# The first expert set's weights and the router's columns, loaded in the last slots of the first attention

## The chip, the cores and the metric

The kernel runs on one core of one Trainium2 chip. The metric is the device time of one execution in microseconds (us). The kernel before took 2045.58 us, the median of three runs (2042.79 to 2046.41). Times inside the kernel come from one profiled execution and are counted from the start of its span.

Five engines work beside each other, each with its own instruction stream: TensorE (PE; its weight loads are shown apart as PEld), VectorE (DVE), ScalarE (ACT), GpSimd (POOL) and SyncE (SP), which only issues transfers. A "q" behind a name (SPq, ACTq) marks the issuing of transfers and other work of that engine's sequencer. Engines wait for each other on semaphores.

## The reference, cut to what matters

Two layers run over x of 8 x 256 tokens x 512 features. Each layer is a gated cross attention and then a gated feed-forward part. The change lies between the first attention and the first feed-forward part:

```python
x = x + tanh(g_xattn[0]) * L0_xattn(layernorm(x), ctx, ...)   # 32 heads, rotary positions
x = x + tanh(g_ffn[0]) * L0_ffn(layernorm(x), ...)            # below
...                                                           # second attention, second routed part

def L0_ffn(x):                       # 2048 tokens, 16 experts, inner width 352
    probs = softmax(x @ w_gate.T)
    top_w, top_i = top_k(probs, 4)
    routed = sum over the 4 chosen experts e of  w_e * (silu(x @ wg[e]) * (x @ wu[e])) @ wd[e]
    shared = silu(x @ sg) * (x @ su) @ sd          # inner width 704
    return routed + shared
```

## The kernel before

**Two stages, one behind the other.** `rope_attention` computes the first attention and `expert_ffn` the first feed-forward part. Each is a block of five instruction streams, and between the blocks all engines meet at a barrier and the semaphores of the first are cleared. In the profile the last instruction of the first block ends shortly before 611 us and the first of the second starts at 612.5 us.

**The attention** runs through slots s = -21 to 132. Slots 0 to 127 each handle one pair of heads of one batch element (16 slots for each of 8 elements). Every engine's program is written out by hand as a loop over s, so the order of work on an engine is fixed by the code. In a slot, ACT copies a transposed tile out of PSUM (`turned_back`, L970), then computes the exponentials of the next pair (`exponentials`, L963), which wait for DVE's row maxima (`top`, L845). PE transposes exponentials (L1158) and computes scores (L1147). The last projection products of the last element (L1072) come in slots 120, 124, 128 and 131.

**Weight splitting inside the attention.** PE multiplies fp32 data as sums of fp32r parts, so every weight is split into a high and a low part. Eighteen sets (two halves of the shared expert, then 16 experts) are cut into 7 pieces each. SP loads a piece to `praw` (L551), POOL splits it (L671, L673) and SP writes both parts to the DRAM tensor `w_parts` (L559, L561). This goes on from slot 2 to the end of the attention. The pieces of set 0 are written first.

**The expert stage** works in units of 128 tokens: units 0 to 15 with set 0, 16 to 31 with set 1, and then 79 routed units. `wh` and `wl` hold high and low parts of three sets in SBUF. The streams at the start of this block are:

- SP: load the router's weights (`gw`, L1424); `weights(0)`: the gate columns of set 0, high and low (L1389), the rest of its rows (L1393) and the last 96 rows of the down weights (the tails, L1397); then zero rows, 17 clearing transfers for `slots`, and the copies of the normed tokens (L1439).
- ACT: issue a load of the routed map (L1715), wait for `gw` and write its high part beside the gate columns (L1742), then `tokens_high` (L1697) of units 0 and 1, then the logits' copy (L1708) and the silu (L1709) of unit 0.
- DVE: `normed(0)`, `normed(1)` (L1780), `dump_tokens` (L1973), `router_low` (L1787), `normed(2)`, `tokens_low(0)` (L1795), `normed(3)`, `tokens_low(1)`, some constants, and `acts(0)` (L1824).
- POOL: clear six tails of `wh` and `wl` (L1495), then `zero`, `empty` and `ent`, then an iota into `empty` (L1500), for which `dump_tokens` waits, and further constants.
- PE: `turn_tokens(0)`, `turn_tokens(1)` (L1575), `gate_products(0)` (L1605), `up_products(0)` (L1618), `turn_tokens(2)`, `gate_products(1)`, `turn_acts(0)` (L1627), `up_products(1)`, `down_products(0)` (L1638), and so on.

`gate_products(0)` waits for both gate transfers and for the router's parts; `up_products(0)` waits for the four transfers of rest and tails. `turn_tokens(1)` writes the PSUM tile that `tokens_low(0)` reads, and waits for it.

Of the kernel before, what the change touches and what calls it, by code (L numbers as in the profile page):

```python
# [15 lines left out]
P = 128  # L16
# [141 lines left out]
class Split:  # L158


    def __init__(self, nc, wg, wu, wd, sg, su, sd):
        self.wg, self.wu, self.wd, self.sg, self.su, self.sd = wg, wu, wd, sg, su, sd
        self.I = wg.shape[2]
        self.shared = sg.shape[1] // self.I
        self.sets = self.shared + wg.shape[0]
        self.rows = (self.I + P - 1) // P
        self.across, self.down = 2 * KD * self.I, self.rows * D
        self.each = KD + self.rows
        self.count = self.sets * self.each
        self.parts = nc.dram_tensor("w_parts", [self.sets, 2, P, self.across + self.down], F32, kind="Internal").ap()  # L170
        assert KD % 2 == 0 and 2 * self.I <= PIECE and D <= PIECE
# [134 lines left out]
def rope_attention(nc, core, x, ctx_d, pos, Wq, Wkv, Wout, bout, g_xattn, g_ffn, placing, table, split):  # L306
# [43 lines left out]
    SECOND_TOKENS = -1  # L350
    maps_W, atoms, eaw, importance, mask_idx = placing
# [45 lines left out]
    with ExitStack() as ctx:  # L397
# [3 lines left out]
        place_sums, place_rows = sb("place_sums", [P, C, E]), sb("place_rows", [P, C], U32)  # L401
# [3 lines left out]
        at_ = lies("atoms", [P, NS // 2], F32, nc.sbuf_base - 4 * KD * D)  # L405
        CS = sb("cs", [P, NT, 2, 2 * 8])
# [3 lines left out]
        xn = sb("xn", [P, BT, D])  # L410
        xT, cT = sb("xT", [P, KD, S]), sb("cT", [P, KC, S])
        rot, tmp = sb("rot", [P, 2, D]), sb("tmp", [P, 2, D])
        hlq, hlk = sb("hlq", [P, 2, H, 2, HD]), sb("hlk", [P, 2, H, 2, HD])
        qT, qS, kT = [sb(n, [P, QUADS, S], F32R) for n in ("qT", "qS", "kT")]
# [57 lines left out]
        phigh_done, plow_done = sem("phigh_done"), sem("plow_done")  # L472
        load_positions, angles, sines, tables = rope_tables(nc, ctx, pos, CS)
# [58 lines left out]
        kview = lambda a: a.rearrange("(k p) n -> p k n", p=P)  # L532

        @block.sync
        def _(eng):
# [184 lines left out]
        def _(eng):  # L720
# [235 lines left out]
        def _(eng):  # L956
# [59 lines left out]
            for s in range(FIRST, LAST):  # L1016
# [197 lines left out]
def expert_ffn(nc, core, w_gate, split, gate, Wq, Wk, Wv, Wkv_dca, Wo, table):  # L1214
# [3 lines left out]
    E, K, I = w_gate.shape[1], 4, split.I  # L1218
# [10 lines left out]
    GATE, UP, DOWN = KD * GE, KD * I, J * D  # L1229
    RAW = GATE + UP + DOWN  # L1230
    NW = 3
# [38 lines left out]
    with ExitStack() as ctx:  # L1270
# [11 lines left out]
        gw = sb("gw", [P, KD, E])  # L1282
# [39 lines left out]
        gw_in, gw_ready = sem("gw_in"), sem("gw_ready")  # L1322
# [20 lines left out]
        def columns(w, at, c, n):  # L1343

            if isinstance(at, int):
                return w[:, at, c:c + n]
# [11 lines left out]
        def loaded(eng, s):  # L1358

            eng.wait_ge(gate_in[s % NW], 32 * (s // NW + 1))  # L1360
            eng.wait_ge(rest_in[s % NW], 64 * (s // NW + 1))

# [14 lines left out]
        def _(eng):  # L1377
            def weights(s):
# [8 lines left out]
                for i, w in enumerate((wh, wl)):  # L1387
                    r, p_ = r32(w[:, s % NW, :]), split.parts[s, i]
                    eng.dma_start(r[:, 0:GATE].rearrange("p (k n) -> p k n", k=KD)[:, :, 0:I],  # L1389
                                  p_[:, 0:KD * I].rearrange("p (k n) -> p k n", k=KD)).then_inc(gate_in[s % NW], 16)  # L1390
                for i, w in enumerate((wh, wl)):
                    r, p_ = r32(w[:, s % NW, :]), split.parts[s, i]
                    eng.dma_start(r[:, GATE:GATE + UP + 2 * D],  # L1393
                                  p_[:, KD * I:2 * KD * I + 2 * D]).then_inc(rest_in[s % NW], 16)
# [29 lines left out]
            eng.dma_start(gw[:, :, :], w_gate.rearrange("(k p) e -> p k e", p=P)).then_inc(gw_in, 16)  # L1424
# [140 lines left out]
        def _(eng):  # L1565
# [116 lines left out]
        def _(eng):  # L1682
# [89 lines left out]
        def _(eng):  # L1772
# [9 lines left out]

            def router_low():

                eng.wait_ge(gw_ready, 1)
                pads = lambda w: w[:, 0, 0:GATE].rearrange("p (k n) -> p k n", k=KD)[:, :, I:GE]
                eng.tensor_tensor(pads(wl), gw[:, :, :], r32(pads(wh)),  # L1787
                                  ALU.subtract).then_inc(gw_ready, 1)
# [189 lines left out]
            router_low()  # L1978
# [1278 lines left out]
def program(nc, x, ctx_1024, fside_BxSx2_0, g_xattn, g_ffn, *args):  # L3257
# [6 lines left out]
    with ExitStack() as ctx:  # L3264
# [8 lines left out]
                       (W, atoms, atom_weights, importance, mask_idx), table, split)  # L3273
        Wq, bq, Wk, bk, Wv, bv, Wkv_dca, bkv_dca, *norms, Wo, bo = attn1
        expert_ffn(nc, core, ffn0[0], split, core.gates[:, 2:3], Wq, Wk, Wv, Wkv_dca, Wo, table)
# [35 lines left out]
```

## Time and profile before

| | us |
|---|---|
| median of three runs | 2045.58 |
| the profiled execution | 2045.0 |
| its span | 2043.3 |
| PE busy | 1836.0 (90%) |
| DVE busy | 1181.0 (58%) |
| POOL busy | 961.7 (47%) |
| ACT busy | 925.6 (45%) |
| mean granted clock of PE, as a share of full speed | 0.947 |

The span is the time from the first to the last instruction in the profile; the execution's own time is 1.7 us longer. Busy time is an average over stages with different limits. PE is the busiest engine, but a busy engine may run at the lower of its two clock levels (1.2 instead of 2.4 GHz), which the profile's PEclk shows as 0.50.

### The profile page before, as it was taken

What the parts mean: (1) busy time and instruction counts of PE and PEld (TensorE: products, weight loads), DVE (VectorE), ACT (ScalarE), POOL (GpSimd) and SP (SyncE); (2) the same over time, 40 slices, a digit from 0 to 9 for tenths busy, and PEclk for the clock granted to TensorE, in tenths of its full rate; (3) what the DMA queues carried; (4) which work ended last, traced back from release to release, by engine and by line L of the source; (5) the groups of instructions that cost most, each with busy time, mean ns of one, the idle gap of its engine ahead of it and who ended that gap; (6) DMA issues with size and microseconds to landing.
All of it is one profiled execution on the core that took longest, in us unless ns stands there. A gap on an engine that the chain in (4) does not pass through costs nothing. (4 is left out here: it accounts for less than half of the span.)

```text
span 2043.3 us, 38716 instructions
## 1 busy us (share of the span) xinstructions
PE 1836.0 (90%) x11488; PEld 1411.4 (69%) x11488; DVE 1181.0 (58%) x2665; ACT 925.6 (45%) x2631; POOL 961.7 (47%) x1018
## 2 busy tenths in 40 slices
PE   5889999999978999999999999994789999886992
PEld 3555666566547999999999999982455566555881
DVE  6866777677654875333333353325777778764445
ACT  5466767676642332233333333321466666640110
POOL 2557877788641364043333443322455555212660
PEclk9789999999998999999999999997899999996996
DMA  9677787778757246589999986533444545539657
GB/s 301 236 230 231 243 279 239 220 240 282 236 170 279 80 132 212 161 233 273 324 328 268 275 261 192 119 59 107 92 109 104 118 100 119 127 104 365 235 163 277
DMA packets 234941, 414.82 MB, mean 203 GB/s; under 512 B 44361, under 2 KB 121457, under 8 KB 228986
## 3 DMA queue, kind: packets, MB, share of 16 engines
q1 hardware_dynamic: 168250, 323.86, 49.7%
q0 software_dynamic: 30592, 62.54, 13.2%
q10 hardware_dynamic: 35904, 25.96, 4.2%
q8 instruction: 106, 1.74, 0.3%
q14 instruction: 89, 0.73, 0.1%
HBM read 211.97 MB, written 157.82 MB: 181 GB/s over the span
## 5 line engine op out<-in xcount | busy, mean ns | idle before, releaser
L963 ACT ACTIVATE a_P<-a_SC,a_nm 128x256 f32<-128x256 f32 x512 | 235.9, 473 | 151.5 <-DVE a_nm L845 150.9
L1543 POOL DMA_INDIRECT b_y_rows<-b_ysb,b_entry x79 | 125.0, 1582 | 334.8 <-ACT b_ysb L1691 185.0
L845 DVE TENSOR_REDUCE a_nm<-a_SC 128x2 f32<-128x512 f32 x256 | 164.7, 685 | 127.8 <-PE a_SC L1147 127.7
L673 POOL TENSOR_TENSOR a_praw<-a_praw,a_phigh 128x704 f32<-128x704 f32 (+2 forms) x126 | 193.8, 1538 | 10.3
L1795 DVE TENSOR_TENSOR b_xl<-b_XT,b_xh 128x512 fp32r<-128x512 f32 x97 | 67.0, 691 | 216.1 <-ACT b_xh L1697 215.7
L1158 PEld LDWEIGHTS a_T<-ident,a_P 128*128 128x128 f32 x1024 | 121.4, 146 | 86.5 <-issue 46.4
L1158 PE MATMUL a_T<-ident,a_P 128*128 128x128 f32 x1024 | 149.5, 285 | 26.8 <-DVE a_PT L857 24.1
L671 POOL CAST a_phigh<-a_praw 128x704 fp32r<-128x704 f32 (+2 forms) x126 | 106.5, 845 | 107.1 <-DMA a_praw<-in_L_ffn_wd 33.4
L1801 DVE TENSOR_TENSOR b_al<-b_AT,b_ah 128x384 fp32r<-128x384 f32 x111 | 61.8, 557 | 152.6 <-ACT b_ah L1702 152.6
L2529 ACT ACTIVATE c_P<-c_SC,c_nm 128x240 f32<-128x240 f32 x256 | 115.7, 457 | 75.6 <-DVE c_P L2400 75.6
L1691 ACT ACTIVATE b_ysb<-b_Y 128x512 f32<-128x512 f32 x79 | 47.3, 599 | 223.1 <-PE b_Y L1638 211.6
L1702 ACT ACTIVATE b_ah<-b_AT 128x384 fp32r<-128x384 f32 x111 | 54.6, 492 | 199.4 <-PE b_AT L1627 199.4
L1522 POOL DMA_INDIRECT b_slots<-b_ysb,b_at_u x64 | 65.5, 1023 | 105.3 <-DVEq L1888 87.0
L963 ACT ACTIVATION_READ_ACCUMULATOR a_P<-a_SC,a_nm 128x1 f32 x512 | 103.9, 203 | 0.0
L1530 POOL DMA_INDIRECT b_xg<-b_xn_rows,b_entry x79 | 78.3, 991 | 53.2 <-issue 22.5
L2394 DVE TENSOR_REDUCE c_nm<-c_SC 128x2 f32<-128x480 f32 x128 | 81.9, 640 | 36.7 <-PE c_SC L2704 36.2
L1638 PE MATMUL b_Y<-b_wh,b_ah 128*128 (+1 forms) x333 | 95.8, 396 | 0.9 <-ACT b_ah L1702 0.9
L1638 PE MATMUL b_Y<-b_wh,b_al 128*128 (+1 forms) x333 | 94.6, 392 | 0.0
L1638 PE MATMUL b_Y<-b_wl,b_ah 128*128 (+1 forms) x333 | 94.3, 391 | 0.0
L2714 PE MATMUL c_T<-ident,c_P 128*128 128x128 f32 x512 | 71.5, 281 | 24.5 <-POOL c_P L2321 15.5
L2714 PEld LDWEIGHTS c_T<-ident,c_P 128*128 128x128 f32 x512 | 57.4, 143 | 51.8 <-POOL c_P L2321 24.4
L1147 PE MATMUL a_SC<-a_kT,a_qT 32*128 32x256 f32 x512 | 82.5, 336 | 11.3 <-DMA a_qS<-a_qT 3.4
(496 smaller groups left out, 4916.4 us busy)
## 6 DMA issues: line engine op xcount, KB each, us to landing
w_parts<-a_phigh SPq DMA_DIRECT2D x72, 352.0 KB, 3.6
w_parts<-a_praw SPq DMA_DIRECT2D x72, 352.0 KB, 4.1
b_wh<-w_parts SPq DMA_DIRECT2D x18, 1216.0 KB, 10.9
b_wl<-w_parts SPq DMA_DIRECT2D x18, 1216.0 KB, 14.4
c_q<-c_qT SPq DMA_DIRECT2D x64, 256.0 KB
c_k<-c_kT SPq DMA_DIRECT2D x124, 128.0 KB
b_wh<-w_parts SPq DMA_DIRECT2D x18, 704.0 KB, 5.2
b_wl<-w_parts SPq DMA_DIRECT2D x18, 704.0 KB, 7.8
```

Source lines behind the costliest of these rows:

```text
L671: eng.tensor_copy(high[:, 0:k * m], raw[:, 0:k * m]).then_inc(phigh_done, 1)
L673: eng.tensor_tensor(raw[:, 0:k * m], raw[:, 0:k * m], r32(high[:, 0:k * m]), ALU.subtract).then_inc(plow_done, 1)
L845: eng.tensor_reduce(nm[:, g % 4, j, :], SC[j][:, :].rearrange("p (t k) -> p t k", t=BT), AX.X, ALU.max, negate=True).then_inc(topped, 1)
L963: e = eng.activation(Pr[:, i, t, :], SC[j][:, t * S:(t + 1) * S], ACT.Exp, bias=nm[:, g % 4, j, t:t + 1], accum_out=den[:, h, t:t + 1])
L1147: m = eng.matmul(SC[j][:, t * S:(t + 1) * S], q[r:r + R, p // 2, t * P:(t + 1) * P], kT[r:r + R, p // 2, :], start=(half == 0), stop=(half ...
L1158: m = eng.transpose(T_[j][:, k * S + t * P:k * S + (t + 1) * P], Pr[:, (2 * g + j) % NP_, t, k * P:(k + 1) * P], core.ident[:, :])
L1530: eng.indirect_dma_start(out=xg[:, row(v), :], out_offset=None, in_=xn_rows, in_offset=bass.IndirectOffsetOnAxis(ap=entry[:, r, 1:2].bitca ...
L1543: eng.indirect_dma_start(out=y_rows, out_offset=bass.IndirectOffsetOnAxis(ap=entry[:, r, 1:2].bitcast(U32), axis=0), in_=ysb[:, v % RING, ...
L1638: m = eng.matmul(Y[v % 2][:, :], a_[:, v % 2, j * P:(j + 1) * P], down_rows(w_, at_unit[v], j), start=(i == 0), stop=(i == 3 * J - 1))
L2394: eng.tensor_reduce(nm[:, g % 4, j, :, 0], v[:, :, 0:MAIN], AX.X, ALU.max, negate=True)
L2529: e = eng.activation(Pr[:, i, t, 0:MAIN], SC[j][:, t * S:t * S + MAIN], ACT.Exp, bias=nm[:, g % 4, j, t, 0:1], accum_out=den[:, h, t, 0:1])
L2714: m = eng.transpose(T[j][:, k * S + t * P:k * S + (t + 1) * P], Pr[:, (2 * g + j) % NP_, t, k * P:(k + 1) * P], core.ident[:, :])
```

## The change

The gate columns of set 0 and the rest of its rows without the tails (2 x 704 KB and 2 x 1216 KB) are no longer loaded at the start of the expert stage, but by ACT in slots 120 to 123 of the attention, one transfer in each. They go to the same SBUF addresses at which `wh` and `wl` of set 0 lie in the next block; in the attention these bytes hold projection weights, token tiles and other tensors that nothing reads any more by then. Tiles in the attention are laid out in another order for this. In slot 120 ACT also waits until the pieces of set 0 are written (semaphores that were reached long before) and issues the load of `gw`. In slot 124 ACT writes the router's high part, and in slot 125 DVE writes its low part. SP waits for the four transfers at the end of the attention. In the expert stage SP's load of `gw`, its four large transfers of set 0, ACT's wait and copy and DVE's `router_low` are gone, and PE's unit 0 waits only for the two tails. `dump_tokens` and POOL's clears stay as they are.

```diff
+                if s == FIRST_SET_AT:                       # ScalarE's stream in the attention; PAIRS * (B - 1) + 8 = 120
+                    is_freed(eng, (B - 1, "k1b"))
+                    n = split.each
+                    for i in range(NRAW):
+                        eng.wait_ge(plow_out[i], 16 * ((n - 1 - i) // NRAW + 1))
+                    for i in range(NHIGH):
+                        eng.wait_ge(phigh_out[i], 16 * ((n - 1 - i) // NHIGH + 1))
+                    eng.dma_start(gw[:, :, :], w_router.rearrange("(k p) e -> p k e", p=P)).then_inc(gw_in, 16)
+                if FIRST_SET_AT <= s < FIRST_SET_AT + 4:
+                    i, rest_ = (s - FIRST_SET_AT) % 2, s >= FIRST_SET_AT + 2
+                    if rest_:
+                        dst = r32(first_set[i][:, split.gate:split.raw - D])
+                        src_ = split.parts[0, i, :, split.up:2 * split.up + 2 * D]
+                    else:
+                        dst = r32(first_set[i][:, 0:split.gate]).rearrange("p (k n) -> p k n", k=KD)[:, :, 0:split.I]
+                        src_ = split.parts[0, i, :, 0:split.up].rearrange("p (k n) -> p k n", k=KD)
+                    eng.dma_start(dst, src_).then_inc(first_in, 16)
+                if s == ROUTER_AT:                          # FIRST_SET_AT + 4
+                    eng.wait_ge(gw_in, 16)
+                    eng.activation(router_columns(0), gw[:, :, :], ACT.Copy).then_inc(gw_high, 1)
...
+                if s == ROUTER_AT + 1:                      # VectorE's stream in the attention
+                    eng.wait_ge(gw_high, 1)
+                    eng.tensor_tensor(router_columns(1), gw[:, :, :], r32(router_columns(0)), ALU.subtract)
...
+            eng.wait_ge(first_in, 16 * 4)                   # SyncE, end of the attention
...
                 for i, w in enumerate((wh, wl)):            # SyncE in the expert stage, weights(s)
+                    if s == 0:
+                        break
...
+                    if s:
+                        eng.dma_start(r[:, GATE:GATE + UP + 2 * D],
+                                      p_[:, KD * I:2 * KD * I + 2 * D]).then_inc(rest_in[s % NW], 16)
...
-            eng.dma_start(gw[:, :, :], w_gate.rearrange("(k p) e -> p k e", p=P)).then_inc(gw_in, 16)
...
-                    eng.wait_ge(gate_in[v // NT], 32)       # TensorE, weights_at
+                    if v >= NT:
+                        eng.wait_ge(gate_in[v // NT], 32)
...
-                if v == 0:
-                    eng.wait_ge(gw_ready, 2)
...
-                    eng.wait_ge(rest_in[v // NT], 64)       # TensorE, up_products
+                    eng.wait_ge(rest_in[v // NT], 64 if v >= NT else 32)
...
-            eng.wait_ge(gw_in, 16)                          # ScalarE, before unit 0
-            eng.activation(wh[:, 0, 0:GATE].rearrange("p (k n) -> p k n", k=KD)[:, :, I:GE], gw[:, :, :],
-                           ACT.Copy).then_inc(gw_ready, 1)
...
             dump_tokens()                                   # VectorE, before unit 0
-            router_low()
```

## Rows read from the trace of the kernel before

**Rows 1.** Waits, all engines, 590 to 660 us: who waited for whom, total, times, longest.

```profile
PE b_XT L1575 <- DVE b_wl L1795: 4.9, 1, 4.9
ACT b_wh L1742 <- DMA b_gw<-in_L_ffn_w_gate: 12.0, 1, 12.0
PE b_U L1618 <- DMA b_wl<-w_parts: 3.9, 1, 3.9
```

**Rows 2.** Timeline of PE, 590 to 650 us: start, duration, instruction, idle before.

```profile
613.38 1.12 PE L1575 MATMUL b_XT<-ident,b_xg 128*128 128x128 f32 x4 [4.54 <-DVE b_xg L1780]
619.43 1.09 PE L1575 MATMUL b_XT<-ident,b_xg 128*128 128x128 f32 x4 [4.94 <-DVE b_wl L1795]
621.27 1.59 PE L1605 MATMUL b_G<-b_wh 128*128 128x368 f32 x4 [0.76 <-DMA b_wl<-w_parts]
...
629.09 1.54 PE L1618 MATMUL b_U<-b_wh 128*128 128x352 f32 x4 [3.92 <-DMA b_wl<-w_parts]
...
632.77 1.06 PE L1575 MATMUL b_XT<-ident,b_xg 128*128 128x128 f32 x4
633.49 1.58 PE L1605 MATMUL b_G<-b_wh 128*128 128x368 f32 x4
...
636.34 0.49 PE L1627 MATMUL b_AT<-ident,b_act 128*128 128x128 f32 x3
636.58 0.89 PE L1618 MATMUL b_U<-b_wh 128*128 128x352 f32 x4
...
638.60 0.85 PE L1638 MATMUL b_Y<-b_wh,b_ah 128*128 128x512 f32 x3
...
641.01 0.91 PE L1605 MATMUL b_G<-b_wh 128*128 128x368 f32 x4
...
643.11 0.49 PE L1627 MATMUL b_AT<-ident,b_act 128*128 128x128 f32 x3
```

**Rows 3.** Windows of 1 us: busy of PE, PEld, DVE, ACT, POOL; PEclk, DMA share, GB/s.

```profile
624.00:625.00 1.00, 1.00 (x5) 0.84 (x3) 0.00 (x0) 0.00 (x0) 0.00 (x0) 0.57 1.13 290
...
628.00:629.00 1.00, 0.00 (x0) 0.00 (x0) 0.00 (x0) 0.00 (x0) 0.00 (x0) 0.64 1.02 346
...
635.00:636.00 1.00, 1.00 (x8) 1.00 (x7) 0.19 (x1) 0.00 (x0) 0.00 (x0) 0.95 1.08 408
```

**Rows 4.** Timelines of POOL, DVE and ACT, 590 to 650 us.

```profile
617.62 0.21 POOL L1500 IOTA b_empty<- 128x16 int32 x1
...
617.86 0.26 DVE L1973 TENSOR_SCALAR b_empty<-b_empty 128x16 int32<-128x16 int32 x1 [3.80 <-POOL b_empty L1500]
...
618.61 0.67 DVE L1795 TENSOR_TENSOR b_wl<-b_XT,b_wh 128x512 fp32r<-128x512 f32 x1
...
617.30 0.26 ACT L1742 ACTIVATE b_wh<-b_gw 128x64 fp32r<-128x64 f32 x1 [12.00 <-DMA b_gw<-in_L_ffn_w_gate]
...
626.69 0.46 ACT L1709 ACTIVATE b_silu<-b_G 128x352 f32<-128x352 f32 x1
```

**Rows 5.** Waits of PE alone, 636 to 1100 us (the whole answer).

```profile
PE b_G L1605 <- issue: 0.6, 1, 0.6
```

**Rows 6.** Issues on SP's queue, 607 to 665 us.

```profile
612.51 0.41 SPq L1424 DMA_DIRECT2D b_gw<-in_L_ffn_w_gate  x1
...
613.52 1.27 SPq L1389 DMA_DIRECT2D b_wl<-w_parts  x1
```

**Rows 7.** Timeline of ACT, 566 to 593 us (slot 120 to 121).

```profile
574.25 0.61 ACT L970 ACTIVATE a_PT<-a_T 128x512 f32<-128x512 f32 x1
575.98 0.48 ACT L963 ACTIVATE a_P<-a_SC,a_nm 128x256 f32<-128x256 f32 x1 [1.12 <-DVE a_nm L845]
```

**Rows 8.** The longest issue on ACT's queue, from its timeline, 1250 to 1298 us.

```profile
1250.08 6.24 ACTq L1715 DMA_DIRECT2D b_mraw<-table  x1
```

**Rows 9.** PE and POOL, 566 to 613 us, and one window of 2 us.

```profile
581.24 0.63 PE L1158 MATMUL a_T<-ident,a_P 128*128 128x128 f32 x4 [1.48 <-DVE a_PT L857]
...
600.42 0.40 POOL L659 COPY a_recw<-a_rec 128x256 f32<-128x256 f32 x1 [3.50 <-DVE a_rec L852]
...
580.00:582.00 2.00, 0.63 (x4) 0.44 (x5) 1.18 (x3) 2.00 (x9) 1.57 (x1) 1.00 1.03 385
```

More of the change, by code:

```diff
@@ L169, in __init__ @@
         self.count = self.sets * self.each
+        self.gate_wide = self.I + wg.shape[0]
+        self.gate, self.up = KD * self.gate_wide, KD * self.I
+        self.raw, self.buffers = self.gate + self.up + self.rows * D, 3
         self.parts = nc.dram_tensor("w_parts", [self.sets, 2, P, self.across + self.down], F32, kind="Internal").ap()
@@ L303, in rope_tables, with rope_attention @@
     return load, angles, sines, tables
-def rope_attention(nc, core, x, ctx_d, pos, Wq, Wkv, Wout, bout, g_xattn, g_ffn, placing, table, split):
+def rope_attention(nc, core, x, ctx_d, pos, Wq, Wkv, Wout, bout, g_xattn, g_ffn, placing, table, split, w_router):
     H, HD = 32, 16
@@ L350, in rope_attention @@
     SECOND_TOKENS = -1
+    FIRST_SET_AT = PAIRS * (B - 1) + 8
+    ROUTER_AT = FIRST_SET_AT + 4
     maps_W, atoms, eaw, importance, mask_idx = placing
@@ L400, in rope_attention @@
         lies = lambda name, shape, dt, at: nc.alloc_sbuf_tensor_at("st_" + name, shape, dt, offset=at)
-        place_sums, place_rows = sb("place_sums", [P, C, E]), sb("place_rows", [P, C], U32)
+        first_set = [nc.alloc_sbuf_tensor_at(f"a_first_set{i}", [P, split.raw], F32R,
+                                             offset=nc.sbuf_base + 4 * i * split.buffers * split.raw) for i in range(2)]
+        core.first_set = first_set
+        first_main = 4 * (split.raw - D)
+        first_at = nc.sbuf_base
         wq, wkv, wo = sb("wq", [P, KD, D]), sb("wkv", [P, KC, 2 * D]), sb("wo", [P, KD, D])
@@ L405, in rope_attention @@
         at_ = lies("atoms", [P, NS // 2], F32, nc.sbuf_base - 4 * KD * D)
+        assert first_at + first_main <= wo_at
+        place_sums, place_rows = sb("place_sums", [P, C, E]), sb("place_rows", [P, C], U32)
         CS = sb("cs", [P, NT, 2, 2 * 8])
@@ L410, in rope_attention @@
         xn = sb("xn", [P, BT, D])
+        gw = lies("gw", [P, KD, w_router.shape[1]], F32, nc.sbuf_base - 4 * BT * D)
         xT, cT = sb("xT", [P, KD, S]), sb("cT", [P, KC, S])
         rot, tmp = sb("rot", [P, 2, D]), sb("tmp", [P, 2, D])
+        assert first_at + 4 * split.buffers * split.raw >= nc.sbuf_base - 4 * 2 * D
         hlq, hlk = sb("hlq", [P, 2, H, 2, HD]), sb("hlk", [P, 2, H, 2, HD])
+        assert first_at + 4 * split.buffers * split.raw + first_main <= nc.sbuf_base
         qT, qS, kT = [sb(n, [P, QUADS, S], F32R) for n in ("qT", "qS", "kT")]
@@ L472, in rope_attention @@
         phigh_done, plow_done = sem("phigh_done"), sem("plow_done")
+        first_in, gw_in, gw_high = sem("first_in"), sem("gw_in"), sem("gw_high")
         load_positions, angles, sines, tables = rope_tables(nc, ctx, pos, CS)
@@ L532, in rope_attention, with router_columns @@
         kview = lambda a: a.rearrange("(k p) n -> p k n", p=P)
+        def router_columns(i):
+            return first_set[i][:, 0:split.gate].rearrange("p (k n) -> p k n", k=KD)[:, :, split.I:]
         @block.sync
@@ L1211, in chosen_part, with expert_ffn @@
     eng.tensor_tensor(gt, a, b, ALU.is_gt).then_inc(sem, c.inc())
-def expert_ffn(nc, core, w_gate, split, gate, Wq, Wk, Wv, Wkv_dca, Wo, table):
-    E, K, I = w_gate.shape[1], 4, split.I
+def expert_ffn(nc, core, split, gate, Wq, Wk, Wv, Wkv_dca, Wo, table):
+    E, K, I = split.sets - split.shared, 4, split.I
     J = 3
@@ L1228, in expert_ffn @@
     GE = I + E
-    GATE, UP, DOWN = KD * GE, KD * I, J * D
-    RAW = GATE + UP + DOWN
-    NW = 3
+    GATE, UP, RAW, NW = split.gate, split.up, split.raw, split.buffers
+    assert GE == split.gate_wide and J == split.rows
     GT = 4
@@ L1281, in expert_ffn @@
         lnsc, lw = core.lnsc, sb("lw", [P, 5, NT])
-        gw = sb("gw", [P, KD, E])
         empty = sb("empty", [P, CLEAR, SLOT])
@@ L1321, in expert_ffn @@
         gate_in, rest_in, routed_in = sems("gate_in", NW), sems("rest_in", NW), sem("routed_in")
-        gw_in, gw_ready = sem("gw_in"), sem("gw_ready")
         mraw_in, high_out, low_out = sem("mraw_in"), sem("high_out"), sem("low_out")
@@ L1343, in columns @@
         def columns(w, at, c, n):
+            if isinstance(at, int) and at == 0 and c < GATE + UP + 2 * D:
+                return core.first_set[0 if w is wh else 1][:, c:c + n]
             if isinstance(at, int):
@@ L1358, in loaded @@
         def loaded(eng, s):
-            eng.wait_ge(gate_in[s % NW], 32 * (s // NW + 1))
-            eng.wait_ge(rest_in[s % NW], 64 * (s // NW + 1))
+            eng.wait_ge(gate_in[s % NW], 32 * (s // NW + (s % NW > 0)))
+            eng.wait_ge(rest_in[s % NW], 64 * (s // NW) + (64 if s % NW else 32))
         def token_parts(v):
@@ L1392, in weights @@
                     r, p_ = r32(w[:, s % NW, :]), split.parts[s, i]
-                    eng.dma_start(r[:, GATE:GATE + UP + 2 * D],
-                                  p_[:, KD * I:2 * KD * I + 2 * D]).then_inc(rest_in[s % NW], 16)
+                    if s:
+                        eng.dma_start(r[:, GATE:GATE + UP + 2 * D],
+                                      p_[:, KD * I:2 * KD * I + 2 * D]).then_inc(rest_in[s % NW], 16)
                     if s < 2:
@@ L1781, in normed @@
                                   ALU.mult, ALU.add).then_inc(xn_ready, 1)
[L1783 to L1788, printed above, removed]
             def tokens_low(v):
@@ L3272, in program @@
         rope_attention(nc, core, x, ctx_1024, fside_BxSx2_0, *attn0, g_xattn, g_ffn,
-                       (W, atoms, atom_weights, importance, mask_idx), table, split)
+                       (W, atoms, atom_weights, importance, mask_idx), table, split, ffn0[0])
         Wq, bq, Wk, bk, Wv, bv, Wkv_dca, bkv_dca, *norms, Wo, bo = attn1
-        expert_ffn(nc, core, ffn0[0], split, core.gates[:, 2:3], Wq, Wk, Wv, Wkv_dca, Wo, table)
+        expert_ffn(nc, core, split, core.gates[:, 2:3], Wq, Wk, Wv, Wkv_dca, Wo, table)
         core.Xa = ctx.enter_context(nc.sbuf_tensor("Xa", [P, NT, D], F32))
```

## The prediction

> **What bounds the kernel now.** I read the page first: PE is busy for 90% of the span, so time can be won only where PE stands still or runs slowly. The windows by stage put such a place at the start of the expert stage, and the waits there [rows 1] name three suspects: ACT's 12.0 us for the router's weights, PE's 4.9 us for DVE, and PE's 3.9 us for the weights of set 0. The 12.0 is a trap: it counts from ACT's last work in the attention, and since the transfer is issued only at 612.51 [rows 6] and ACT goes on at 617.30 [rows 4], no more than 4.8 us of it belongs to the load. What counts is PE's own timeline [rows 2]. After the barrier it transposes unit 0 at 613.38, stands until 619.43, transposes unit 1, starts the gate products at 621.27 when the low gate columns land, and after them stands 3.92 us until 629.09, when the low rest lands. Unit 0's up products then take until 632.77, and the first gate products of unit 1 until 636.34. From 636 to 1100 us PE waits for nothing but 0.6 us of issue [rows 5]. So what PE wins before 636 us should be kept through those units, since later loads hang on PE's own progress.
>
> The windows of 1 us [rows 3] add the clock. PE's granted clock is at half (1.2 GHz) when the gate products start, rises within 624 to 625 us (0.57 over that microsecond, so at about 624.9), while the gate products run, falls back in 628 to 629 us after the stall, and rises again at the very start of 635 us (0.95). The second stall therefore costs twice: the time itself, and half speed after it until 635.
>
> **Removed: the wait for gate columns and router.** PE may start the gate products of unit 0 when its tokens are split. That is where the first gain stops short. DVE writes the low tokens at 618.61, and before that in its program stands `dump_tokens`, which starts at 617.86 because POOL's iota starts only at 617.62 behind its clears [rows 4]. The change touches neither. The router's load ended at about the same moment by accident: ACT's wait and DVE's wait were late together, and with the first gone the second is there in full. All that goes from this chain is `router_low`, some 0.1 us. PE's transposes of unit 1 go from 619.43 to 619.3. At half clock the next products follow 0.72 us behind them (632.77 to 633.49 [rows 2]), so at 620.0 instead of 621.27. The gain so far is 1.25 us, not the 5 or so that the waits suggest.
>
> **Removed: the wait for the rest.** At half clock the up products take 629.09 to 632.77 = 3.68 us; the gate products with 368 columns for 352 take 3.68 x 368/352 = 3.85. They end at 620.0 + 3.85 = 623.9. The up products now wait for the two tails only (192 KB each). These wait for POOL's first two clears, over by 613.8, and have 10 us for what stood in one line with all of set 0 before. Cost nothing; if this cover is gone, each microsecond of lateness past 623.9 is lost.
>
> **The clock.** In the trace the rise at 624.9 came 5.5 us after PE's work began at 619.43, and the rise at 635.05 came 6.0 us after 629.09. PE now works without a pause from 619.3, with more work before 624.9 than it had, so I take the rise at the same 624.9. The up products do 1.0 of their 3.68 us at half clock, and the rest at full speed: 2.02 us for all (636.58 to 638.60), so 0.73 x 2.02 = 1.47. They end at 626.4 instead of 632.77. The transposes of unit 2 take half of 0.72, so unit 1's gate products start at 626.7, and at full speed take 2.10 us (641.01 to 643.11) for 2.85 (633.49 to 636.34 [rows 2]). They end at 628.8 instead of 636.34: **7.5 us** saved. Nothing else is late there: the silu of unit 0 ended 2.0 us after its gate products [rows 2, 4], so at 626.0, and DVE's 0.5 us behind the up products is done at 627.2, before PE wants it at 628.8. Had the clock stayed low until 635 as well, U and G of units 0 and 1 would end at 623.9 + 3.68 + 0.72 + 3.85 = 632.2, a gain of 4.1 us. Had it risen at 623, another 0.95 us would come.
>
> The Trainium skill (TensorE: Matmul & The Clock Gate, What's actually happening) says that the gate's moment of change depends on where the first matmul falls and varies from run to run. The rows agree in that the two rises come 5.5 and 6.0 us after work starts; by that rule the rise may come about half a microsecond to either side, which moves the sum by some 0.25 us, since half of each microsecond at half clock is lost.
>
> **Added in the attention.** Five issues, some ten waits that are long met, one ACT copy and one DVE subtraction. Slot 120's exponentials end just before 574.25, and the issues stand behind them and ahead of the copy L970 [rows 7]. What queues behind them on ACT is that copy and then the next exponentials, for which DVE and PE wait. But these exponentials start 1.12 us later than they could, waiting for DVE. So up to 1.1 us per slot is hidden. Slot 120 holds the router's issue (0.41) and one gate issue; large issues took 0.50 to 1.27 on SP [rows 6]. I take 0.41 + 0.50 + 0.4 for the waits = 1.3, so 0.2 shows, and 0.5 to 0.9 in slots 121 to 123, which is hidden. In those slots PE also has idle time of 1.48 us before its transposes, which end in a wait for DVE [rows 9]. ACT's copy (0.26) lies in an idle stretch. DVE's subtraction (0.22) is on the chain that PE waits for: 0.1 to 0.2. Together 0.5 us; bounds 0 and, if each issue holds as long as the worst in the trace (6.24 [rows 8]), 4 x (6.24 - 1.1) = 20.6 us. I take the low end, since SP issued these same transfers back to back, with 1.27 for the one shown [rows 6], and here they are 3.6 us apart. A gain below nothing is not excluded either: slots' ends shift against the clock's changes, some 1 us to either side.
>
> **The bytes.** 3840 KB, 3.9 MB, move into 574 to 590 us. At the 385 GB/s of a full window [rows 9] that is 10.2 us of transfer time. The pieces share the engines: their loads and stores get later, SP and POOL with them. POOL's last widened denominators had been free to start 3.50 us earlier [rows 9]; and the block ends only near 611. So a lag of 3.5 us is free for POOL. The four transfers start in four slots, 1.8 to 3.2 us of work each in 3.6, and the pieces' last loads come after 590, when these are done. Cost 0.
>
> The Trainium skill (DMA: Bandwidth & Descriptors, Issuing engines are not separate DMA queues) says that transfers from ScalarE run on the same 16 engines as SyncE's and interleave, so another issuer saves only issue time. It speaks against the change where the share is full, as in 580 to 582 us [rows 9]; by it all 10 us of them come on top of the pieces' traffic, and what does not fit in idle windows shows as POOL's lag.
>
> **The sum.** 7.5 - 0.5 = 7.0 us off the profiled execution's 2045.0, which gives 2038.0. It lies 0.6 under the median of 2045.58; on that median the forecast is 2038.6 us.
>
> **Rivals.** (a) Full gain: POOL's clears and `dump_tokens` don't hold DVE, and the token split follows the first transposes. These end at 614.5, and with ACT's and DVE's 1.3 us the second transposes start at 616, 3.3 us sooner; the gain is 11, the time 2034.8. For it: the 12.0 and 4.9 of [rows 1]. Against it: the program order and 617.86 [rows 4]. (b) Small gain: the clock rises later, or tails land after 623.9, with what remains of 7.5 near 4.1 to 5: 2041. For it: two periods of half clock in the trace; against it, that continuous work should not make the rise later. (c) Nothing: issue holds or a late POOL eat 4 to 10 us in the attention: 2042 to 2048. (d) Slower: ACT's issues in slots 121 to 123 hold as in [rows 8], because the pieces keep the DMA engines full (1.03 in 580 to 582). The price is 3 x (6.24 - 1.1) = 15.4 us less 7.5: 2053.5. It decides from a hold of 3.6 us in each slot on. Against it: the same transfer took 1.27 us to issue from SP [rows 6], a third of the hold that decides.
>
> **How the numbers follow.** My forecast, with 2036.5 to 2040.8 as its own range, gets 0.72; (a) 0.04; (b) 0.11; (c) 0.08; (d) 0.05. The range of 2035.0 to 2042.0 leaves out (d), most of (c) and part of (a). What a measurement of this kernel tells from no change is about 0.2%, 4.1 us, so a time under 2041.5 is faster: 0.72 + 0.04 + most of (b) and a little of (c) = 0.87. Within 0.2%: 0.08. Slower: 0.05.
>
> **What would show it.** In the changed kernel DVE's `dump_tokens` still starts 5.4 us after the block's start and `tokens_low(0)` right behind it; PE's gate products of unit 0 start 7.5 us after the block's start (8.8 before), the up products follow without a wait, and PEclk rises once within them and stays. Unit 0's L1627 comes 16.3 us after the block's start instead of 23.8. The attention's last instruction ends within 1 us of 610.8. A block that ends over 3 us later, or ACT issues above 1.3 us each, would prove (c) or (d); PE starting the second transposes before 617 would prove (a). A second fall of the clock before L1627 of unit 0 would prove (b).

## The result and the profile after

| | before | after |
|---|---|---|
| median of five runs | 2045.58 us | 2032.25 us (2031.29 to 2038.17) |
| ratio | | 0.9942, interval 0.9922 to 0.9962 |
| profiled execution, span | 2045.0, 2043.3 | 2031.29, 2029.6 |
| expert block's first instruction | 612.5 | 606.6 |
| from there to unit 0's L1627 (L1670 after) | 23.8 | 15.3 |

The kernel is 13.3 us faster by the medians, 8 to 16 by the interval; 7.0 were forecast, and the time lies below the forecast range. It is nearest to rival (a)'s 2034.8, but what rival (a) needed did not happen, as the lines below show. The last two rows of the table already say where to look: the start of the expert block gave 8.5 us, and 5.9 us were there before it began; behind both, 0.7 us were lost again.

PE after, timeline (start, duration, instruction, idle before). This answers to [rows 2]:

```profile
607.45 1.12 PE L1619 MATMUL b_XT<-ident,b_xg 128*128 128x128 f32 x4 [4.56 <-DVE b_xg L1820]
613.35 1.09 PE L1619 MATMUL b_XT<-ident,b_xg 128*128 128x128 f32 x4 [4.79 <-DVE b_wl L1828]
614.09 2.80 PE L1648 MATMUL b_G<-a_first_set,b_wh 128*128 128x368 f32 x8
...
617.46 1.45 PE L1661 MATMUL b_U<-a_first_set,b_wh 128*128 128x352 f32 x8
...
619.40 0.60 PE L1619 MATMUL b_XT<-ident,b_xg 128*128 128x128 f32 x4
619.76 1.59 PE L1648 MATMUL b_G<-a_first_set,b_wh 128*128 128x368 f32 x8
...
621.86 0.49 PE L1670 MATMUL b_AT<-ident,b_act 128*128 128x128 f32 x3
```

Both stalls for transfers are gone, and from 613.35 on PE does not stop. The wait that stays is the one for DVE, and behind it stands the order that the forecast named: POOL's iota, `dump_tokens`, the token split, as in [rows 4]. `dump_tokens` starts 5.3 us after the block's start (5.4 forecast).

```profile
611.68 0.21 POOL L1544 IOTA b_empty<- 128x16 int32 x1
...
611.92 0.26 DVE L2006 TENSOR_SCALAR b_empty<-b_empty 128x16 int32<-128x16 int32 x1 [3.79 <-POOL b_empty L1544]
...
612.53 0.67 DVE L1828 TENSOR_TENSOR b_wl<-b_XT,b_wh 128x512 fp32r<-128x512 f32 x1
```

The clock, in a window of 1 us (PEclk is the third number from the end), answers to [rows 3]. The value is 0.50 before this window, 0.54 in it and 1.00 after it, so the clock rises once, at about 616.9:

```profile
616.00:617.00 1.00, 1.00 (x5) 1.00 (x5) 0.08 (x2) 0.00 (x0) 0.00 (x0) 0.54 0.78 262
```

In the attention, ACT's issues and the exponentials of the slot after the first of them (compare [rows 7]):

```profile
565.96 0.43 ACTq L1071 DMA_DIRECT2D st_gw<-in_L_ffn_w_gate  x1
...
566.43 0.52 ACTq L1080 DMA_DIRECT2D a_first_set<-w_parts  x1
...
568.62 0.47 ACT L986 ACTIVATE a_P<-a_SC,a_nm 128x256 f32<-128x256 f32 x1 [0.97 <-DVE a_nm L865]
...
569.22 0.39 ACTq L1080 DMA_DIRECT2D a_first_set<-w_parts  x1
...
573.26 0.34 ACTq L1080 DMA_DIRECT2D a_first_set<-w_parts  x1
...
576.72 0.34 ACTq L1080 DMA_DIRECT2D a_first_set<-w_parts  x1
```

No issue took more than 0.52 us, and the issues lie beside the exponentials in the profile, not between them: ACT's sequencer ran ahead of its arithmetic. The exponentials still waited 0.97 us for DVE, against 1.12 before. From ACT's PSUM copy in slot 120 to the one in slot 128 it is 29.6 us, and it was 29.9. So no cost is seen there. The pieces did give way. POOL's last copy, which had waited 3.50 us for DVE [rows 9], now has no wait at all: POOL stood 4.23 us for the load of an earlier piece. The copy comes 1.7 us after ACT's last PSUM copy (592.87), where before it came 0.1 us ahead of it, so the free 3.5 us were used up and more. PE takes up the denominators at 596.64, without a wait:

```profile
587.91 0.61 POOL L691 CAST a_phigh<-a_praw 128x512 fp32r<-128x512 f32 x1 [4.23 <-DMA a_praw<-in_L_ffn_wd]
...
594.53 0.39 POOL L679 COPY a_recw<-a_rec 128x256 f32<-128x256 f32 x1
...
596.64 0.38 PE L1216 MATMUL a_O<-ident,a_recw 128*128 128x128 f32 x2
```

### The profile page after: what moved, and what is told of

Read it like the earlier page. It is cut to its first block and busy times, and to the rows that moved or that the text cites. A ratio compares the mean times of both kernels' runs of the same rounds, so it can differ in the third digit from the quotient of the medians.

```text
span 2029.6 us, 38719 instructions
## 1 busy us (share of the span) xinstructions
PE 1825.5 (90%) x11488; PEld 1403.7 (69%) x11488; DVE 1181.2 (58%) x2665; ACT 925.7 (46%) x2631; POOL 961.4 (47%) x1018
## 3 DMA queue, kind: packets, MB, share of 16 engines
q8 instruction: 106, 1.74, 0.3%
## 5 line engine op out<-in xcount | busy, mean ns | idle before, releaser
L693 POOL TENSOR_TENSOR a_praw<-a_praw,a_phigh 128x704 f32<-128x704 f32 (+2 forms) x126 | 193.4, 1535 | 10.3
L1681 PE MATMUL b_Y<-b_wh,b_ah 128*128 (+1 forms) x301 | 88.3, 396 | 0.9 <-ACT b_ah L1745 0.9
L877 DVE COPY a_PT<-a_T 128x512 f32<-128x512 f32 x128 | 87.0, 680 | 1.0 <-PE a_T L1201 1.0
L1681 PE MATMUL b_Y<-b_wh,b_al 128*128 (+1 forms) x301 | 87.4, 392 | 0.0
## 6 DMA issues: line engine op xcount, KB each, us to landing
b_wl<-w_parts SPq DMA_DIRECT2D x17, 1216.0 KB, 13.8
```

Of the source, the lines that this page charges most:

```text
L693: eng.tensor_tensor(raw[:, 0:k * m], raw[:, 0:k * m], r32(high[:, 0:k * m]), ALU.subtract).then_inc(plow_done, 1)
L877: eng.tensor_copy(PT[:, 2 * g % NPT, :, :].rearrange("p t s -> p (t s)"), T_[0][:, :]).then_inc(pt_done[0], 1)
L1681: m = eng.matmul(Y[v % 2][:, :], a_[:, v % 2, j * P:(j + 1) * P], down_rows(w_, at_unit[v], j), start=(i == 0), stop=(i == 3 * J - 1))
```

## The experiments

In what follows "the part" is the time from the expert block's start to unit 0's transposed activations: 23.8 us before, 15.3 with the change.

**The changed kernel again, twice** (no edit; the second time beside `dump_again` and `warm` below).

> The changed kernel once more, unchanged. In its first profile the expert block started 5.9 us earlier than before the change (606.6 for 612.5), and the gain was made before slot 120, where PE's clock was at half in four stretches (17 us in all between 115 and 552 us) before the change and in none after. Theory 1 (chance): these stretches come and go from run to run; this profile shows a block start anywhere from 606 to 613 us, times from 2031 to 2038 us, and the part from the block's start to unit 0's transposed activations stays at 15.3 us (14.5 to 16.5). Theory 2 (the new placing of tiles in the attention makes it quicker): the block starts at 606 to 607 again, and all times lie near 2032 us.

> The changed kernel, a third time, beside the two below on one chip. By the two profiles so far: 15.3 to 15.4 us from the expert block's start to unit 0's transposed activations and 1423 to 1424 us from there to the end of the span; the block's start anywhere from 606 to 613 us. Median 2035 to 2038 us.

The medians were 2037.83 (ratio 0.9954, 0.9937 to 0.9971) and 2035.26 us (0.9950, 0.9932 to 0.9968), beside 2046.27 and 2045.14 for the kernel before in the same rounds. The block started at 612.6 and at 611.8, not at 606.6, with the same program. The windows of 105 to 545 us, in which the change adds or removes no instruction, show the granted clock that goes with it: of before, of the first profile after, and of the two repeats, in this order.

```profile
105.00:545.00 440.00, 418.48 (x3167) 265.56 (x3168) 309.13 (x609) 304.88 (x1049) 328.30 (x299) 0.98 0.78 242
```

```profile
105.00:545.00 440.00, 416.34 (x3208) 265.05 (x3200) 312.65 (x616) 309.14 (x1066) 333.50 (x303) 1.00 0.79 245
```

```profile
105.00:545.00 440.00, 416.77 (x3181) 264.56 (x3175) 310.28 (x612) 305.35 (x1055) 328.56 (x300) 0.99 0.78 241
```

```profile
105.00:545.00 440.00, 417.64 (x3168) 264.43 (x3168) 309.06 (x611) 305.25 (x1053) 328.60 (x300) 0.98 0.78 241
```

In the same 440 us the first profile got through more instructions (3208 matmuls for 3167) at a clock of 1.00. The 41 matmuls more are 5.7 us at the rate of before (an estimate: 3167 in 440 us). So the 5.9 us are chance of that execution.

What one fall of the clock costs can be read where the program is the same. In the first repeat the clock is at half from about 599.3 to 602.7, in the second it is not, and PE's four projection products show it:

```profile
599.26 3.56 PE L1115 MATMUL a_W<-a_wo,a_aT 128*128 128x512 f32 x4
```

```profile
600.12 1.88 PE L1115 MATMUL a_W<-a_wo,a_aT 128*128 128x512 f32 x4
```

From slot 128's PSUM copy to the block it is then 13.7 us instead of 12.1. In the profile of before, the clock is at half for four such stretches between 106 and 506 us, 3 to 7 us each; in the first profile of the change there is none in 105 to 541 us.

The second repeat is also a close copy of the forecast, since here the clock rose late:

```profile
618.56 1.09 PE L1619 MATMUL b_XT<-ident,b_xg 128*128 128x128 f32 x4 [4.79 <-DVE b_wl L1828]
619.30 2.80 PE L1648 MATMUL b_G<-a_first_set,b_wh 128*128 128x368 f32 x8
...
628.10 0.49 PE L1670 MATMUL b_AT<-ident,b_act 128*128 128x128 f32 x3
...
624.00:625.00 1.00, 1.00 (x6) 1.00 (x6) 0.00 (x0) 0.99 (x2) 0.00 (x0) 0.80 0.70 239
```

The part is 628.1 - 611.8 = 16.3 us, which is the number forecast, with a rise at 624.4, 12.6 us after the start (12.4 assumed).

**Only the placing of tiles.** The kernel before, with the attention's tiles in the changed order:

```diff
+        first_set = [nc.alloc_sbuf_tensor_at(f"a_first_set{i}", [P, split.raw], F32R, offset=...) for i in range(2)]
-        place_sums, place_rows = sb("place_sums", ...), sb("place_rows", ...)   # ahead of wq, wkv, wo
+        place_sums, place_rows = sb("place_sums", ...), sb("place_rows", ...)   # behind them
```

> The kernel before with nothing but the tiles of the attention in the changed order; all loads stay where they were. Theory 1 (chance): the time is that of before, 2043 to 2047 us, the block's start varies with the half-clock stretches, and from there to unit 0's transposed activations it takes 23.8 us. Theory 2 (placing): the block starts near 606.6 us and the kernel takes 2039 to 2040 us.

Median 2047.74, ratio 1.0002 (0.9985 to 1.0018); the block starts at 614.1, and the part is 23.0 us. The placing gives nothing, and theory 2 is out. The part is 0.8 us shorter than in the profile of before with the same stage program: here the clock did not rise within the gate products but 4.1 us into the work behind the second stall (6.0 before). So the 23.8 itself varies by about that much.

**Only the gate columns and the router moved.** The two rests are loaded by SP in the expert block again.

```diff
-                if FIRST_SET_AT <= s < FIRST_SET_AT + 4:
+                if FIRST_SET_AT <= s < FIRST_SET_AT + 2:
...
-                    if s:
-                        eng.dma_start(r[:, GATE:GATE + UP + 2 * D], ...)
+                    dst = r[:, GATE:GATE + UP + 2 * D] if s else r32(core.first_set[i][:, GATE:GATE + UP + 2 * D])
+                    eng.dma_start(dst, ...)
```

> Of the changed kernel, only the two gate loads (704 KB each) and the router stay in the attention; the two transfers of the rest (1216 KB each) go back to SyncE in the expert block. If each wait is worth what the rows say: gate products start 7.5 us after the block's start, PE then waits 1 to 2 us for the low rest, which lands some 4 us sooner than before since 1.4 MB are gone from ahead of it (12.8 us after the start for 16.6), and unit 0's activations are transposed about 17 to 18 us after the start: 2 us slower than the whole change, 6 faster than before. Rival: the rest lands as late as before (16.6), because the bytes behind it take the freed time; then the clock falls again and the kernel is 6 to 7 us slower than the whole change.

Median 2039.51, ratio 0.9967 (0.9953 to 0.9982). The block starts at 612.4:

```profile
625.37 2.71 PE L1660 MATMUL b_U<-a_first_set,b_wh 128*128 128x352 f32 x8 [1.39 <-DMA b_wl<-w_parts]
...
631.15 0.49 PE L1669 MATMUL b_AT<-ident,b_act 128*128 128x128 f32 x3
```

The up products start at 12.9 us (12.8 expected), and the part is 18.7: 5.1 us less than before. That is a little later than expected, because the clock rose only after this short wait, at about 628.2, 15.8 us after the start. The part is 3.3 us longer than in the first two profiles of the whole change and 2.4 longer than in the third, for a wait of 1.39 us.

**Only the rests and the router moved.** The mirror image: SP loads the gate columns in the expert block.

```diff
-                if FIRST_SET_AT <= s < FIRST_SET_AT + 4:
+                if FIRST_SET_AT + 2 <= s < FIRST_SET_AT + 4:
...
-                    if s == 0:
-                        break
-                    r, p_ = r32(w[:, s % NW, :]), split.parts[s, i]
+                    r, p_ = r32(w[:, s % NW, :]) if s else r32(core.first_set[i][:, :]), split.parts[s, i]
```

> Of the changed kernel, the two rests (1216 KB each) and the router stay in the attention; the two gate loads (704 KB each) go back to SyncE at the start of the expert block. If unit 0's start is held by the token split behind GpSimd's clears, the gate columns, now first in an empty line, are there by 7.5 us after the block's start, and all is as in the whole change: gate products at 7.5, unit 0's activations transposed at 15.3 us, 8.5 less than before. Rival: the gate loads themselves take 8.8 us as before, the gate products start at 8.8 and unit 0's activations are transposed at 16 to 17.

The block starts at 608.65.

```profile
617.35 2.82 PE L1645 MATMUL b_G<-a_first_set,b_wh 128*128 128x368 f32 x8 [0.85 <-DMA a_first_set<-w_parts]
...
626.16 0.49 PE L1667 MATMUL b_AT<-ident,b_act 128*128 128x128 f32 x3
```

The rival was right: PE starts on the gate columns 8.7 us after the block's start, even though they are first in SyncE's line and the rests are gone, and the part is 17.5 (16 to 17 expected). The median was 2039.61, ratio 0.9987 (0.9968 to 1.0005), too wide to tell by itself. The halves of the change give 5.1 and 6.3 us of the part, both together 7.5 to 8.5. They overlap: either half alone leaves one clock rise where there were two, 15.8 and 13.8 us after the start (22.6 before), and both together bring it to 10.3 to 12.6.

**Only the order, no move.** The kernel before, with the first token split ahead of everything that waits for POOL or for the router's load.

```diff
                 normed(v)
-            dump_tokens()
-            router_low()
...
                     tokens_low(u + 2)
+                if u == -2:
+                    dump_tokens()
+                    router_low()
```

(and ScalarE's wait for `gw` with its copy behind its first `tokens_high`).

> The kernel before (all loads in the expert block), with VectorE's dump_tokens and router_low behind the first token split, and ScalarE's wait for the router behind its first tokens_high, so that neither GpSimd's clears nor the router's load holds the split of unit 0. If set 0's loads are by then the bound: second transposes at 3.5 us after the block's start, gate products at 8.8 still, unit 0's activations at 23 to 24, time as before. If the clears were all that held it: gate products near 4.2 and 3 us or more gained.

Median 2045.6, ratio 1.0000 (0.9980 to 1.0019). The block starts at 610.2:

```profile
613.66 1.09 PE L1575 MATMUL b_XT<-ident,b_xg 128*128 128x128 f32 x4 [1.50 <-DVE b_wl L1796]
619.16 1.60 PE L1605 MATMUL b_G<-b_wh 128*128 128x368 f32 x4 [4.41 <-DMA b_wl<-w_parts]
...
634.12 0.49 PE L1627 MATMUL b_AT<-ident,b_act 128*128 128x128 f32 x3
```

The second transposes come 3.5 us after the start instead of 6.9, and the time goes straight into the wait for the gate columns (9.0 us after the start; 8.8 before). The part is 23.9. Before the change there were two waits, one hidden behind the other.

**The order on top of the change**, run twice: `dump_tokens` moves behind the first token split, as above.

> The changed kernel with VectorE's dump_tokens moved from ahead of tokens_low(0) to right behind it, so that the first token split no longer stands behind GpSimd's clears. If that wait was what held the gate products: PE's second transposes start about 3.5 us and the gate products 4.2 us after the block's start instead of 7.5, and the kernel is 1.7 to 3.3 us quicker than the whole change, by how early the clock rises. If the first split was held by something else, the start stays at 7.5 and the time is that of the whole change.

> The kernel with dump_tokens behind the first token split, a second time: 11.9 us to unit 0's transposed activations, 1419 to 1420 us from the block's start to the end, and a median 2 to 4 us below the changed kernel's in the same rounds. If the 3 us between the first medians were chance, the part of the block is 11.9 again but the medians are equal.

Medians 2034.73 (ratio 0.9947, 0.9928 to 0.9966) and 2032.08 (0.9937, 0.9912 to 0.9962): 3.1 and 3.2 us below the changed kernel in the same rounds. The first profile, whose block starts at 611.1:

```profile
614.60 1.09 PE L1619 MATMUL b_XT<-ident,b_xg 128*128 128x128 f32 x4 [1.50 <-DVE b_wl L1828]
615.34 2.79 PE L1648 MATMUL b_G<-a_first_set,b_wh 128*128 128x368 f32 x8
...
623.05 0.49 PE L1670 MATMUL b_AT<-ident,b_act 128*128 128x128 f32 x3
```

Gate products at 4.2 us, part 11.9 us; in the second profile 4.2 and 12.9 (11.9 expected), with the clock rising 3.4 and 5.6 us after the second transposes began. What gave nothing alone gives 3.1 us once the loads are out of the way. It is the fastest of the versions in its own rounds. The intervals against the kernel before overlap with the changed kernel's; that it beats it rests on two pairs of medians and on the part.

**The loads twice.** In slots 124 to 127 ACT issues the four transfers again, to the same places.

```diff
+                if FIRST_SET_AT + 4 <= s < FIRST_SET_AT + 8:
+                    i, rest_ = (s - FIRST_SET_AT) % 2, s >= FIRST_SET_AT + 6
+                    if s == FIRST_SET_AT + 4:
+                        eng.wait_ge(first_in, 16 * 4)
...                                                  # dst and src_ as in the change
+                    eng.dma_start(dst, src_).then_inc(first_in, 16)
```

> The changed kernel with the four loads issued a second time by ScalarE, in slots 124 to 127, to the same places: 3.9 MB more through the last slots. From the PSUM copy of pair 119 to that of pair 127 the profiles show 29.9 us before, 29.6 and 29.9 with the change, and from there to the expert block 12.0 or 13.7. If issues and bytes are free there: 29.6 to 30.0 and 12.0 to 13.8 again. If the bytes cost by sharing the DMA engines with the weight pieces: the pieces' last loads, GpSimd's last copy and the block's start come 2 to 6 us later.

The block starts at 622.45. POOL's last piece and copy, then PE's products that need that copy:

```profile
605.64 0.61 POOL L691 CAST a_phigh<-a_praw 96x512 fp32r<-96x512 f32 x1 [5.03 <-DMA a_praw<-in_L_ffn_wd]
...
607.53 0.39 POOL L679 COPY a_recw<-a_rec 128x256 f32<-128x256 f32 x1
...
608.02 0.66 PE L1227 MATMUL a_O<-ident,a_recw 128*128 128x128 f32 x2 [3.45 <-issue]
608.61 3.64 PE L1234 MATMUL a_O<-a_PT,a_V 128*32 128x256 f32 x32
```

From slot 120's copy to slot 128's it is 30.7 us (29.9), and from there to the block 21.8 (12.0 to 13.7). So bytes do cost there, by the path expected: the last pieces come late, POOL's copy behind them, and PE stands still and then works at half clock (3.64 us for the 32 products, 1.93 in the changed kernel). This profile's copy came 6.9 us after slot 128's PSUM copy and the block some 8 us late, where 2 to 6 were expected. The median, 2039.66 (0.9975, 0.9958 to 0.9993), stands against 2032.25 to 2037.83 for the changed kernel, in other rounds; the profiled execution (2048.85) was the slowest of its ten, so most lost less.

**SyncE as the issuer.** The block of waits and issues moved word for word from ScalarE's to SyncE's slot loop.

> The changed kernel with the waits, the load of the router's columns and the four loads issued by SyncE in the same slots instead of ScalarE. If the issuer doesn't matter, the slots 119 to 127 take 29.6 to 30.0 us, the block's part up to unit 0's activations 15.3, and the time is that of the changed kernel. Rival: behind SyncE's waits for the weight pieces the loads start later, or the pieces' stores behind the issues do, and the block starts 1 to 4 us later.

Median 2036.62, ratio 0.9977 (0.9958 to 0.9995). The slots took 29.8 us, the part was 15.4, the block started at 610.7. SP's issues of the gate pair and rests took up to about 1.7 us, which nothing waited for. In the slots and in the part the issuer makes no difference, and the rival is not seen. The median is 7.5 us under that of the kernel before in the same rounds (2044.1), for 8.4 and 9.9 in the two repeats of the change, too close to tell apart.

**PE kept busy.** On top of the version with the order: 48 transposes of the identity that nothing reads.

```diff
+            for _ in range(28):                          # TensorE, end of the attention
+                eng.transpose(O[:, 0:P], core.ident[:, :], core.ident[:, :])
...
+            busy(8)                                      # the same into Y[0], ahead of unit 0's transposes
...
+                if u == -2:
+                    busy(12)                             # between unit 0's and unit 1's
```

> As the one with dump_tokens behind the first split, with transposes of the identity added on PE that nothing reads: 28 at the attention's end, 8 ahead of unit 0's and 12 between unit 0's and unit 1's, so that PE is busy where it stood still around the block's start. If the half clock after the block's start follows from that standing still, the clock rises sooner than 7.1 us after the start (3 to 5), and unit 0's activations are transposed at 10 to 11 us instead of 11.9: 1 to 2 us gained. If the idle time that remains (the barrier, near 4 us) decides, the rise stays near 7 and nothing is gained; if the added work delays PE's own, the gate products start after 4.2 us and it is slower.

The block starts at 611.05. The last line is the clock in a window of 1 us; it is 1.00 in every window from 600 to 640 us.

```profile
606.07 3.28 PE L1245 MATMUL a_O<-ident 128*128 128x128 f32 x28
...
614.48 1.60 PE L1650 MATMUL b_G<-a_first_set,b_wh 128*128 128x368 f32 x8
...
621.06 0.49 PE L1672 MATMUL b_AT<-ident,b_act 128*128 128x128 f32 x3
...
611.00:612.00 1.00, 0.91 (x9) 0.94 (x10) 0.91 (x2) 0.00 (x0) 0.95 (x2) 1.00 0.00 0
```

The part falls to 10.0 us; the gate products run at full clock from 3.4 us on. But the 28 transposes ran until 609.3, past DVE's last work, and held the barrier: from slot 128's copy to the block it is 14.9 us where 12.0 to 13.7 were usual. The median, 2039.78 (0.9966, 0.9945 to 0.9986; 2026.42 to 2044.22), is no gain but 7.7 us above that of `dump_again` in the same rounds; 1 to 2 us less were expected. The profile shows where some of it went. From the part's end to the end of the span it takes 1413.2 us, for 1408.3 in `dump_again`, and before 978.9 PE stands 2.55 us for SP, which signals that the weights of a later set are loaded, and works at half clock behind it:

```profile
978.89 1.54 PE L1650 MATMUL b_G<-b_wh,b_xh 128*128 x4 [2.55 <-SPq L1450]
```

`dump_later` has the same wait with 1.21 us, `dump_again` and the three profiles of the change have none. So what PE wins early can be lost again at a later load. That full clock over the block's start follows from keeping PE busy is shown; why the median is so much higher is not.

## Why the prediction was wrong

**The start of the expert block: the mechanism right, the gain up to 1.0 us too small.** Each step of it is in the trace. The gate products start at 7.5 us after the block's start in all three profiles, as forecast (8.8 before), because POOL's clears and `dump_tokens` hold the token split. Rival (a), the full gain, is out: that wait is there with 4.79 us, and taking it away was worth another 3.1 us. That the first median lies near its 2034.8 is luck. The up products follow with no wait, so the tails were in time. DVE's `acts(0)` waited for the silu in the first profile (619.6), but was done at 620.2, before PE wanted it at 621.86. What was mis-sized is the clock: "I take the rise at the same 624.9", that is 5.5 us after PE's continuous work began. It came 3.6 us after it in the first profile (613.35 to 616.9), and 5.8 in the third (618.56 to 624.4). The third gave the forecast part of 16.3 us to the tenth, the others 15.3 and 15.4. So the term was 7.5 to 8.5 against the 23.8 of before, and the forecast sat at its low end. Rival (b)'s later rise did not come: the latest was 12.6 us after the start, for 12.4 assumed, and the clock did not fall again before L1670. The bound of half a microsecond to either side, taken from the Trainium skill's page (TensorE: Matmul & The Clock Gate, What's actually happening), was too narrow: these two rises differ by 2.2 us.

**The attention: cost 0 instead of 0.5.** The issues took 0.34 to 0.52 us each and ran beside ACT's arithmetic. Slots 120 to 128 took 29.6, 29.9 and 30.2 us in the three profiles of the change, and 29.8 to 29.9 in the three that have the attention's instructions of before. Rivals (c) and (d) are out: the hold of [rows 8] did not occur. The Trainium skill (DMA: Bandwidth & Descriptors, Issuing engines are not separate DMA queues) says that transfers run on the same 16 DMA engines and interleave, whichever engine issues them. The runs agree: with SyncE as issuer the part was 15.4 us and the slots took 29.8, and a second set of bytes from ScalarE delayed SyncE's pieces. The bytes of the first set cost nothing that shows, but they took most or all of the 3.50 us that POOL's last copy had to spare: its wait is none, 0.31 and 0.74 us in the three profiles.

**What failed: the range left no room for the clock over the attention.** The step that failed is "slots' ends shift against the clock's changes, some 1 us to either side"; it measured 5.9 us in the first profile. Over ten further profiles (the doubled loads left out) the expert block starts from 607.2 to 614.1 us, by no order of versions: the unchanged attention gave 612.5, 614.1 and 610.2, the changed one 606.6, 612.6 and 611.8. Between 105 and 545 us PE has some twenty short waits, and the clock falls behind some of them in one execution and not in the next: before, a wait of 2.60 us for POOL that ended at 157.9 had a fall behind it, and in the first profile of the change the same wait took 3.06 us and had none. That profile had no fall from 105 to 541 us. That is 5.9 of the 13.7 us between the two first profiled spans. Only the first of the five executions was profiled; that the two others near 2032 us were quick for the same reason is inferred, not shown. With the repeats, the changed kernel's 24 times have a median of 2036.1, 9.0 us under the 2045.14 of the kernel before in the rounds of the second repeat. That lies within the range; the median of the first five did not, and I had set the range from the profile's structure without a term for it, though the trace of before showed falls to half clock which I did not price. Of these 9.0 us the part explains 7.5 to 8.5; what the rest is, no run settles.

The rest of the kernel hardly moved: from the part's end to the end of the span it is 1407.0 us before, and 1407.7, 1408.2 and 1406.2 in the three profiles of the change.

## What to carry to other kernels

Behind a barrier, follow the bound engine's own order: a long wait for a load can hide an equally long one for something else, and then either edit alone shows little and the two together much (0 alone, 3.1 us on top). Price a stall of TensorE with the half clock that follows it, and give that rise a spread of 2 us, as it had here. Before a gain is ascribed to an edit, compare the stretch ahead of it between the profiles: what differs there, where the programs are the same, is chance, and it belongs in the range.

## What the runs showed of the hardware that was not expected

- With the same program, TensorE's rise to full clock came 3.6 to 5.8 us after its continuous work began. In the one profile with a gap of 1.39 us within that work it came only 9.0 us after the work began and 2.9 after the gap.
- Transposes that nothing reads kept the clock at full speed over the barrier, a pause of 1.74 us for TensorE: the gate products then took 2.1 us (614.48 to 616.59) instead of 3.4 (614.09 to 617.46).
- ScalarE issues transfers while its arithmetic runs: for the issues of 0.34 to 0.52 us no loss shows.
- The two gate transfers of 704 KB, first in SyncE's line at 608.65, with only the map and two tails issued within the next 2 us, still let TensorE start only 8.7 us after the block's start.
